# The first expert layer in 40 tiles instead of 47, eight of them shared by two experts, with the second down weights fetched from HBM

## The reference

```
logits = x @ router_weight.T + router_bias
top_val, top_idx = top_k(logits, 4);  top_val = softmax(top_val)
gate_up = einsum('th,ehd->etd', x, gate_up_proj) + gate_up_proj_bias
gate = min(gate, 7); up = clip(up, -7, 7); glu = gate * sigmoid(1.702 * gate)
out = einsum('etd,edh->eth', (up + 1) * glu, down_proj) + down_proj_bias
out = (out * router_scores).sum(experts)
```

## Time and profile before

| | |
|---|---|
| runs | 424.31, 425.56, 426.42 us (median 425.56) |
| span of the profiled execution | 422.5 us (first to last instruction; the page gives no time of its own for it beside the three runs) |
| TensorE busy | 407.8 us (97%) |
| VectorE busy | 330.4 us (78%) |
| ScalarE, POOL busy | 233.1 us, 216.9 us |
| layer one's tiles on TensorE | first gate/up at 39.15 us, last at 173.82 us |

### The profile page before, as it was taken

One profiled execution on the slowest core, in us unless ns is written; L12 is line 12 of the kernel. 1 busy time (PEld: TensorE's weight loads), 2 busy tenths in 40 slices (PEclk: granted clock), 3 DMA queues, 4 the chain that ended last, 5 costly groups with the idle time before them and its releaser, 6 DMA issues.

```text
span 422.5 us, 10072 instructions
## 1 busy us (share of the span) xinstructions
PE 407.8 (97%) x3213; PEld 321.5 (76%) x3213; DVE 330.4 (78%) x1121; ACT 233.1 (55%) x592; POOL 216.9 (51%) x208
## 2 busy tenths in 40 slices
PE   8999999999999999989999989999999999999995
PEld 4856999999999999856766668548877786565684
DVE  5876899999987666678999999847688774545896
ACT  3273233333433454589999972554777766633731
POOL 2114487888842322067786720067877740577710
PEclk9899999999999999969999999999999999999999
DMA  6947688889999998729977978023556553333322
GB/s 222 393 167 266 196 265 268 289 256 311 297 316 286 303 314 277 216 62 245 193 152 176 226 269 294 1 67 97 170 182 188 178 173 101 111 101 103 99 62 74
DMA packets 42275, 84.17 MB, mean 199 GB/s; under 512 B 7137, under 2 KB 27105, under 8 KB 41585
## 3 DMA queue, kind: packets, MB, share of 16 engines
q1 hardware_dynamic: 30656, 60.99, 44.1%
q0 software_dynamic: 9936, 20.85, 19.6%
q10 hardware_dynamic: 1632, 1.71, 1.2%
HBM read 65.81 MB, written 15.60 MB: 193 GB/s over the span
## 4 chain that ended last, share of the span: by engine, by line
PE 89%; DVE 7%; issue 2%; DMA 1%; ACT 1%; ACTq 0%; DVEq 0%
PE ps L1173 20%; PE ps L1189 9%; PE ps L1124 7%; PE ps L1370 7%; PE ps L1293 5%; PE ps L1151 5%; PE ps L1268 4%; PE ps L952 3%; PE ps L968 3%; PE ps L1381 3%; PE ps L1110 3%; PE ps L1162 2%; PE ps L971 2%; PE ps L941 2%; PE ps L1338 2%
## 5 line engine op out<-in xcount | busy, mean ns | idle before, releaser
L549 POOL DMA_INDIRECT til<-xn_rows,gidx x71 | 70.7, 996 | 86.4 <-PE ps L1162 38.9
L1173 PEld LDWEIGHTS ps<-til,experts 128*128 128x128 f32 x752 | 91.0, 192 | 3.7 <-issue 1.5
L1173 PE MATMUL ps<-til,experts 128*128 128x128 f32 x752 | 91.8, 275 | 0.1
L714 ACT ACTIVATE til<-ps 128x256 f32<-128x256 f32 x47 | 18.0, 383 | 69.8 <-PE ps L1162 69.8
L839 ACT ACTIVATE til<-til,mxs 128x128 f32<-128x128 f32 (+1 forms) x128 | 49.0, 452 | 0.0
L1189 PE MATMUL ps<-experts,til 128*128 x188 | 48.4, 381 | 0.0
L762 ACT ACTIVATE til<-ps,wtile 128x256 f32<-128x256 f32 x95 | 42.0, 468 | 3.7 <-PE ps L1153 2.4
L1795 DVE CUSTOM_DVE_ANT_0 til<-ps,cst 128x128 f32<-128x128 f32 (+1 forms) x128 | 37.8, 351 | 5.2 <-PE ps L1268 4.4
L1189 PEld LDWEIGHTS ps<-experts,til 128*128 128x128 f32 x188 | 32.1, 190 | 2.8 <-issue 0.3
L600 POOL DMA_INDIRECT rou<-sorted_rows,slotu x16 | 20.5, 1283 | 25.8 <-DMA sorted_rows<-til 19.4
L1126 PE MATMUL ps<-xn,til 128*64 128x192 f32 x192 | 33.8, 329 | 0.0
(11 more groups left out here) (247 smaller groups left out, 936.8 us busy)
## 6 DMA issues: line engine op xcount, KB each, us to landing
experts<-in_gu SPq DMA_DIRECT2D x47, 512.0 KB, 5.4
sorted_rows<-til SPq DMA_DIRECT2D x95, 128.0 KB, 1.9
experts<-in_gu SPq DMA_DIRECT2D x8, 768.0 KB
experts<-in_dn SPq DMA_DIRECT2D x4, 1024.0 KB, 12.4
experts<-in_dn SPq DMA_DIRECT2D x8, 384.0 KB
experts<-att SPq DMA_DIRECT2D x44, 32.0 KB
til<-xn_rows,gidx POOLq DMA_INDIRECT x71
xr<-in_x SPq DMA_DIRECT2D x2, 512.0 KB, 4.2
```

Of the source, the lines that this page charges most:

```text
L549: po.indirect_dma_start(to, None, xn_dram[s.n], bass.IndirectOffsetOnAxis(ap=gidx[:, t:t + 1], axis=0))\
L1173: mm = pe.matmul(ps[:, b0, m * P:(m + 1) * P], gw[:, j, k * w + m * P:k * w + (m + 1) * P], xgT[:, j % 2, k, :], start=(k == 0), stop=(k = ...
```

## The change

Layer one's slots are now rounded up to half tiles of 64 rows: NT0 = 40. 32 tiles hold one expert (WHOLE0). Eight hold two half tiles of two experts (MIXED0), for an expert whose last 64 rows or less are left over. They are taken in groups of five steps, the fourth of each group being the mixed one (tiles 3, 8, 13, ... 38 in the order of work; `tile_at` gives the place in the lists).

- A mixed tile takes two slots of gate/up weights, and is computed as rows: two bias matmuls with a one-hot column (`selc`) as the stationary side, then four matmuls of 64 rows by 512 columns. `gate_rows` is VectorE's part, `turn_rows_back` turns the result on TensorE at lag 3, `copy_rows` copies it to `hT` on ScalarE.
- `down` of a mixed tile has four matmuls of 64 rows. The first half's weights are read from `dn0_sb`, the second half's from `dn_other`, which SP fetches from HBM (256 KB) in `other_down(t)`, in iteration t.
- `gw` has six slots, and SP works five steps ahead instead of four. The two new slots lie in `att`, where `xnT0` was, so the second waits for the last wide projection.
- The routing gets the half tiles' arithmetic: six more operations in the chain, and a joint reduction that finds the owners of whole and half tiles.
- The hidden work moves: rotations at tiles 5, 8, 10, 13, 15, 18, 20, 23; heads at 14 to 24 and 25 to 35; the waits for the heads at 27 and 37; BIAS_TILE 28, and all its matmuls in bank 5.
- Semaphores are renamed or folded into the engines' chains (`s_tab`, `s_rst`, `s_rec`, `s_sil`, `s_x1n`, `h1_ready`); the waits stand where they stood.

The diff, cut to its core:

```diff
-NT0, NT1 = tiles_needed(E0, P), tiles_needed(E1, HALF_ROWS)
+NT0, NT1 = tiles_needed(E0, HALF_ROWS), tiles_needed(E1, HALF_ROWS)
+MIXED0 = E0 // 2
+WHOLE0 = NT0 - MIXED0
+STEPS0, MIXED_AT = 5, 3
+def mixed(i):
+    return i % STEPS0 == MIXED_AT
+def tile_at(i):
+    g, j = divmod(i, STEPS0)
+    return WHOLE0 + g if j == MIXED_AT else (STEPS0 - 1) * g + j - (j > MIXED_AT)
+def slots_at(i):
+    j = i % STEPS0
+    return (MIXED_AT, MIXED_AT + 1) if j == MIXED_AT else (j + (j > MIXED_AT),)
+        gw = [big[:, n * 1024:(n + 1) * 1024] for n in range(4)] + [att[:, n * 1024:(n + 1) * 1024] for n in (6, 7)]
+        dn_other = til[:, 3072:3584]
-        BIAS_TILE = 35
+        BIAS_TILE = 28
+        WEIGHT_TILE = 19
+        ROTATED = (5, 8, 10, 13, 15, 18, 20, 23)
+        HEADS_AT = (14, 25)
+        VALUES_AT = (27, 37)
...
+            def tile_weight(i):
+                g = i // STEPS0
...
+                if i >= STEPS0:
+                    sp.wait_ge(L[0].gu_done, i - STEPS0 + 1)
+                for n, j in enumerate(slots_at(i)):
+                    if g == 0 and j == 4:
+                        sp.wait_ge(L[0].wide_done, NTT)
+                    e = sp.snap(halves[g % 2][n] if mixed(i) else now[tile_at(i) % 4], min_val=0, max_val=E0 - 1)
+                    sp.dma_start(gw[j], gu0[:, bass.ds(e, 1), :].rearrange("p o n -> p (o n)")).then_inc(L[0].w_full[j], 16)
+            def other_down(i):
+                g = i // STEPS0
+                if g == 0:
+                    sp.wait_ge(L[0].lists, 3)
+                else:
+                    sp.wait_ge(L[0].y_done, i - STEPS0 + 1)
+                e = sp.snap(halves[g % 2][1], min_val=0, max_val=E0 - 1)
+                sp.dma_start(dn_other, dn0[:, bass.ds(e, 1), :].rearrange("p o n -> p (o n)")).then_inc(L[0].dn_full, 16)
...
                 for t in range(s.NT + 2):
-                    if s.n == 0 and t + 4 < s.NT:
-                        tile_weight(t + 4)
+                    if s.n == 0 and t + STEPS0 < s.NT:
+                        tile_weight(t + STEPS0)
+                    if s.n == 0 and t < s.NT and mixed(t):
+                        other_down(t)
                     if s.n == 0 and t == s.NT - 5:
                         weights_ahead()
-                    if s.n == 0 and (16 <= t < 27 or 28 <= t < 39):
-                        place_heads(t // 28, t - (16, 28)[t // 28])
+                    for half, at in enumerate(HEADS_AT if s.n == 0 else ()):
+                        if at <= t < at + 11:
+                            place_heads(half, t - at)
                     if t >= 2:
                         store(t - 2, (t - 2) % 4)
...
                 for t in range(4, s.NT):
                     gather(t)
-                    if s.n == 0 and t == 7:
+                    if s.n == 0 and t == ROTATED[0]:
                         po.wait_ge(s.lists, 3)
...
-                    if s.n == 0 and t in (33, 44):
-                        a = t // 44
+                    if s.n == 0 and t in VALUES_AT:
+                        a = VALUES_AT.index(t)
                         po.wait_ge(s_heads[a], 16 * 32)
...
+                def copy_rows(i, j):
+                    if not mixed(i):
+                        return
+                    ac.wait_ge(s.rows_turned, i // STEPS0 + 1)
+                    ac.wait_ge(s.y_done, i - 1)
+                    ac.activation(hT[:, j % 2, :, :], ps[:, 4, 0:D].rearrange("p (k t) -> p k t", k=KD), ACT.Copy).then_inc(s.rows_copied, 1)
...
+                    if mixed(t):
+                        h = 2 * tile_at(t)
+                        for c in range(2):
+                            pe.matmul(ps[c * HALF_ROWS:(c + 1) * HALF_ROWS, b0, :], selc[:, h + c:h + c + 1].broadcast_to([96, HALF_ROWS]), gub_bf, start=True, stop=False)
                     pe.wait_ge(s.xgT_ready, t + 1)
+                    for n in slots_at(t):
+                        pe.wait_ge(s.w_full[n], 16 * (t // STEPS0 + 1))
+                    if mixed(t):
                         for k in range(KD):
+                            for c, n in enumerate(slots_at(t)):
+                                rows = slice(c * HALF_ROWS, (c + 1) * HALF_ROWS)
+                                mm = pe.matmul(ps[rows, b0, :], xgT[:, j % 2, k, rows], gw[n][:, k * w:(k + 1) * w], start=False, stop=(k == KD - 1))
...
+                def turn_rows_back(t, j):
+                    if not mixed(t):
+                        return
+                    g = t // STEPS0
+                    pe.wait_ge(s.rows_gated, g + 1)
...
+                    for k in range(KD):
+                        mm = pe.transpose(ps[:, 4, k * P:(k + 1) * P], ubuf[:, j % 2, k * P:(k + 1) * P], ident)
+                    mm.then_inc(s.rows_turned, 1)
...
+                    if mixed(t):
+                        pe.wait_ge(s.rows_copied, g + 1)
+                        pe.wait_ge(s.dn_full, 16 * (g + 1))
+                        e = pe.snap(first_half[g % 2][0], min_val=0, max_val=s.E - 1)
+                        for k in range(s.KF):
+                            pe.matmul(ps[0:HALF_ROWS, 6 + j % 2, 0:D], hT[:, j % 2, k, 0:HALF_ROWS], dn[:, bass.ds(e * (s.KF * D) + k * D, D)],
+                                      start=(k == 0), stop=(k == s.KF - 1))
+                            mm = pe.matmul(ps[HALF_ROWS:P, 6 + j % 2, 0:D], hT[:, j % 2, k, HALF_ROWS:P], dn_other[:, k * D:(k + 1) * D],
+                                           start=(k == 0), stop=(k == s.KF - 1))
...
-                    run_tiles(s, [(1, 1, up), (0, 1, turn), (0, 4, experts), (0, 1, begin), (1, 1, weights), (1, 1, bias_rows), (3, 1, first_heads), (3, 1, down)])
+                    run_tiles(s, [(3, 1, turn_rows_back), (1, 1, up), (0, 1, turn), (0, 1, experts), (0, 1, begin), (1, 1, weights), (1, 1, bias_rows), (3, 1, first_heads), (3, 1, down)])
...
+                if s.n == 0:
+                    over = odd[:, 0:E]
+                    ve.tensor_tensor(over, ranks[:, NTT, :], nts[:, 0:E], ALU.is_gt).then_inc(s_dve, 1)
+                    ve.tensor_tensor(past, ranks[:, 0:NTT, :], nts[:, 0:E].unsqueeze(1).broadcast_to([P, NTT, E]), ALU.is_ge).then_inc(s_dve, 1)
...
+                    ve.tensor_tensor_scan(odds, ones_e[:, 0:E], over, -2.0 * NT0, ALU.mult, ALU.add).then_inc(s_dve, 1)
...
+                    link(ve.scalar_tensor_tensor(out=jump, in0=odds, scalar=-float(HALF_ROWS), in1=enda[:, 0:E], op0=ALU.mult, op1=ALU.subtract))
+                    ve.tensor_tensor(past, past, jump.unsqueeze(1).broadcast_to([P, NTT, E]), ALU.mult).then_inc(s_dve, 1)
...
+                    link(ve.tensor_tensor(lg, lg, past, ALU.add))
...
+                def gate_rows(t, j):
+                    ve.wait_ge(s.gu_done, t + 1)
+                    g, u = gbuf[:, j % 2, :], ubuf[:, j % 2, :]
+                    ve.tensor_scalar(g, ps[:, 2 + j % 2, 0:F], LIMIT, None, ALU.min).then_inc(s.g_ready, 1)
+                    ve.tensor_scalar(u, ps[:, 2 + j % 2, F:2 * F], 1.0, LIMIT + 1.0, ALU.add, ALU.min).then_inc(s.u_ready, 1)
+                    ve.wait_ge(s.u_ready, t + 1)
+                    link(ve.scalar_tensor_tensor(out=u, in0=u, scalar=1.0 - LIMIT, in1=g, op0=ALU.max, op1=ALU.mult))
+                    ve.wait_ge(s.sig_ready, t + 1)
+                    ve.scalar_tensor_tensor(out=u, in0=sig[:, j % 2, :], scalar=1.0, in1=u, op0=ALU.add, op1=ALU.mult).then_inc(s.rows_gated, 1)
```

More of the change, by code:

```diff
@@ L70, in constants @@
     c[:, C_HALF:C_HALF + 1] = 2 * (p % HALF_ROWS) + p // HALF_ROWS + 1
+    is_half = (p >= 2 * WHOLE0) & (p < 2 * NT0)
+    c[:, C_WHOLE:C_WHOLE + 1] = np.where(is_half, p // 2, p) + 1
+    c[:, C_ODD:C_ODD + 1] = np.where(is_half, -p, 1000)
     c[:, C_PART:C_PART + 1] = np.where((p >= 32) & (p < 96), -1.0, 0.0)
@@ L230, in build_program @@
         texi = sb("texi", [P, P], i32)
-        selc = sb("selc", [96, NT0], bf16)
-        bcol = sb("bcol", [P, 4, NT0])
+        selc = sb("selc", [96, 2 * NT0], bf16)
+        bcol = sb("bcol", [P, 4, WHOLE0])
+        odd = sb("odd_parts", [P, 4 * E0])
+        owner = sb("owners", [P, 2])
         wq = sb("wq", [P, NTT, 2, 3, 2], fp16)
@@ L299, in __init__ @@
                 if n == 0:
-                    self.w_full = [sem(f"gate_up_weights_{j}") for j in range(4)]
+                    self.w_full = [sem(f"gate_up_weights_{j}") for j in range(FETCHED)]
                     self.bcol_done = sem("bias_columns_picked")
@@ L798, in tiles @@
                 if s.n == 0:
-                    run_tiles(s, [(0, 1, turn), (0, 1, last_wide), (4, 1, weigh), (1, 1, gate), (1, 1, place_heads), (2, 1, bias_rows)])
+                    run_tiles(s, [(3, 1, copy_rows), (0, 1, turn), (0, 1, last_wide), (4, 1, weigh), (1, 1, gate), (1, 1, place_heads), (2, 1, bias_rows)])
                 else:
@@ L922, in _ @@
             before = [pe.alloc_register(f"expert_before{j}") for j in range(4)]
+            first_half = [[pe.alloc_register(f"first_half{g}_{j}") for j in range(2)] for g in range(2)]
```

(37 more changed lines are left out.)

177 lines of the change are left out of this document (95 added, 82 removed).

## The result

The changed kernel takes 455.99 us (median of 4 runs, 454.07 to 458.62) against 424.94 us (4 runs) for the kernel before: a ratio of 1.0734, 95% interval 1.0688 to 1.0779. That is slower by 31 us, where 16 were predicted, and it lies 1 us outside the range. The profiled execution's span is 453.8 us (before 422.5).

The account below looks back on a forecast made before the run. TensorE was taken as the bound, late arrivals adding one to one. Terms -20.1 + 7.8 + 1.4 + 15.6 + 8.0 + 0.8 + 2.5 = +16.0 us on 425.6 gave 441.6 us, range 427 to 455.

Parts of the forecast that it names:

- Tiles and mixed steps: Layer one on TensorE: seven steps of 2.87 us go, -20.1 us; eight mixed steps cost 0.97 more each, +7.8 us.
- Routing: Routing before the tiles: six more VectorE instructions, less smaller equality tables, delay TensorE's first list matmul by 1.4 us.
- The late fetch: Mixed tiles' down: second weights land late, TensorE waits 1.9 us at three tiles, 2.4 at four, 0.3 at one: +15.6 us.
- The clock: TensorE's granted clock falls after the idle time at `turn(38)`; 5 us at half speed cost +2.5 us.
- rival 3: TensorE's clock falls at every late fetch, 3.2 us each, seven make +22: 464 us; chance 0.10.
- The gather of tile 38: POOL waits for the heads before gathering this tile, so TensorE waits +8.0 us at `turn(38)`.
- The gather of tile 6: POOL's gather early in layer one: lands about when it is due, counted as nothing.
- Tile 28: Its gather comes late behind the heads: +0.8 us, or +3.2 if the fetch in step 26 is in time.
- Rival 2: Second down weights' fetch is in time, gathers behind the heads are not: +2.8 us, 428.4 us; chance 0.13.
- Rival 1: Fewer tiles pay: fetch lands before `down(t)`, heads early enough for tile 38; -10.9 us, 414.7 us; chance 0.12.

Follow-up runs that it names:

- the first run with filled idle time: The changed kernel with ten unused bf16 matmuls before TensorE's wait for the fetch in six mixed tiles: 452.21 us, ratio 1.0644 to the kernel before.
- the run with the early fetch: The changed kernel with the second down weights fetched two iterations earlier, ahead of that iteration's gate/up weights: 442.45 us, ratio 1.0399 to the kernel before.
- the version with everything in time: The changed kernel with the fetch two iterations earlier, GpSimd's head waits after tiles 31 and 39, heads before early loads, rotations from tile 7: 416.58 us.
- the copy: The version with everything in time, but ScalarE copies the second down weights from dn0_sb in place of the HBM fetch: 413.30 us, ratio 0.9733.

## Why the prediction was right in direction and short by half

1. **Tiles and mixed steps: right.** A whole step stayed at 2.87 us, and a cycle without waits is 15.33 us: 5 x 2.87 + 0.98, where 0.97 was predicted, from layer two's rows.
2. **Routing: too high.** VectorE's chain is 1.1 us longer, where 1.4 were predicted, but the first gate/up starts at 39.26 against 38.98 us. The step that failed is that TensorE "waits for VectorE's L1561 there". The bracket of the earlier trace rows names VectorE as the releaser, but VectorE's first table was done at 23.87 us (23.18 + 0.69) and TensorE loaded the list's weights at 25.03, behind matmuls that it had anyway: 1.16 us to spare. Now the table is done at 25.03 and the weights are loaded at 25.12, so the longer chain just fits. The 0.3 that are left lie within what the variants show, where the first gate/up starts between 38.66 and 39.55. Before, and after:

```profile
23.18 0.69 DVE L1561 TENSOR_TENSOR rou<-iota_mid,slot_mid 128x1024 f16<-128x1024 f16 x1
25.46 0.46 PE L1013 MATMUL ps<-til,rou 128*128 128x47 f16 x12
...
24.35 0.68 DVE L1688 TENSOR_TENSOR rou<-iota_mid,slot_mid 128x1024 f16<-128x1024 f16 x1
25.12 0.10 PEld L1073 LDWEIGHTS ps<-til,rou 128*128 128x128 f16 x1 [0.24 <-DVE rou L1688]
25.54 0.65 PE L1073 MATMUL ps<-til,rou 128*128 128x40 f16 x12
```

3. **The late fetch: right in mechanism, 15.6 us predicted, 18.8 measured.** At tile 8 issue (1.67 us into the step, predicted 1.8) and due time (5.25, predicted 5.24) were right. The landing was not: predicted at 7.1, it came at 8.3, and TensorE started at 8.55. Two terms of it were too small. The first gate/up weights, taken as there 4.3 us after their issue, took 5.7 at tile 8 and 4.6 at tile 13. "The second 512 KB and the fetch's 256 KB behind it need 1.28 and 0.64 us", together 1.92, at the 411 GB/s of a window with nothing but loads; they took 1.9 at tile 8, but 3.4 at tile 13 and 2.2 to 3.0 at the four behind it. While the fetch is under way, stores and gathers are under way too, and all of them together get 325 GB/s. Nor did the waits fall as the sum has them: tile 3, counted with 1.9, waits for nothing, since TensorE stood at `turn(6)` until 60.12 while the fetch landed at 58.6, and the four tiles with heads, put down from 3.3 to 2.4 each, waited 3.0 on average. By the limit of 358 GB/s that the Trainium skill gives (DMA: Bandwidth & Descriptors, Specifications) the waits would come to an estimated 19.1 us. Its total is the nearer one, but the kernel before moved 427 GB/s from 14 to 18 us, and a window of 1 us in the first run with filled idle time has 432, so it isn't that limit which was met. The Trainium skill (Perfetto Trace Analysis, Roofline) lets a core alone reach about 435 GB/s. With that the 427 and 432 agree. The landing of the first weights (L485) and of the fetch (L494), for tile 8 and for tile 13, and the window of the kernel before:

```profile
DMA to landing us min/median/max: 5.7/5.7/5.7
DMA to landing us min/median/max: 6.6/6.6/6.6
...
DMA to landing us min/median/max: 4.6/4.6/4.6
DMA to landing us min/median/max: 6.6/6.6/6.6
...
14.00:18.00 4.00, 4.00 (x13) 2.99 (x13) 3.55 (x28) 0.43 (x2) 0.00 (x0) 0.59 1.03 427
```

4. **The clock: the term that failed most.** Of the 13 us between the sum of +16 and the +29 added up above, 11.5 are here. I took +2.5 once and gave the fall at every late fetch a chance of 0.10. The reason given against it, that TensorE "is full before and after" the gap, was wrong: full work around it did not help. It fell after all six waits, and after both gathers: some +14 us. That is as rival 3 had it, but at 1.6 each, not 3.2, and beside waits larger than its sum counted.
5. **The gather of tile 38: 4.79, predicted 8.0.** The heads' way was as described: POOL waited 19.40 us for them.

```profile
190.70 0.20 POOL L617 MEMSET att<- 128x64 f32 x1 [19.40 <-DMA experts<-att]
190.79 0.91 POOL L618 MEMSET att<- 128x960 f32 x1
191.86 0.95 POOL L600 DMA_INDIRECT til<-xn_rows,gidx  x1 [0.16 <-issue]
```

   Against the start of step 37 (183.31) the gather went out at 8.55, predicted 10.0. The sync engine isn't held by TensorE's waits, and the last heads went out 0.19 us into that step (183.50), predicted 3.4; but POOL woke 7.2 us behind them, where 5.4 were taken. And the gather was due 1.9 us later, since that step ran mostly at half clock. The two make the 3.2 us. With the fetch in time it waits 9.55.
6. **The gather of tile 6: counted as nothing, 3.39 us and a fall of 1.6.** "The gather of tile 6 lands about when it is due" took a landing of about 2.7 us. POOL issued it at 54.25, behind the rotation of tile 5, while two weights and a fetch issued from 52.33 to 53.49 were under way, and TensorE could start on it only 5.9 us later.
7. **Tile 28: +0.8 predicted, none measured.** The waits of TensorE before it (four of them) gave the heads time. Without these it is 5.2 to 8.7 us, more than the 3.2 predicted for that case.

Rival 2 ("the fetch is in time, the gathers are not", 428.4) is the run with the early fetch: 442.45. It too was short by tile 28, by `turn(6)` and by the clock at each. Rival 1 (nothing late, 414.7) is the version with everything in time: 416.6, or 413.3 with the copy. The rivals' sums held where they had only TensorE's own work in them.

At the layer's end (its last down matmuls, at 208.75 against 179.26 us) the change is 29.5 us behind, at the end of the span 31.3. The version with everything in time loses 1.1 us there too. The granted clock is 0.50 for 10.2 us at the start of the attention, in both, against 6.8 us before. Whether that is the cause was not tried.

## What to carry to other kernels

Removing work from an engine that is the bound pays only if what it fetches keeps the old distance: count for each transfer how many bytes stand before it in its queue, and what else the DMA engines carry in that time, not the rate and the landing times of a quieter window. Price a wait of TensorE at its length plus what half the clock costs behind it. And when a wait is removed, look at once for the next thing that had been living from it: here the gathers, then the fetches themselves.

## What the runs showed of the hardware

- TensorE's granted clock fell to 0.50 behind every single wait of 2.32 us or more between full stretches of layer one (2.32 to 9.55 us, 31 of them in eight kernels), and behind none of the single waits up to 2.25 us (2.19, 2.20, 2.21 and 2.25 among them). These are too few to call the figure between them a limit: two short waits close together (0.64 and 1.20) also made it fall once, and at the start of the attention, with matmuls of 16 rows around it, it fell in every run within 3.1 us of a wait of 1.41, in some behind a second one of up to 1.00.
- Behind waits of up to 5 us it mostly came back 3 to 4 us after its fall, at 1.5 to 1.6 us lost. Six times it took near 7 us and cost 2.4 to 3.0 (behind waits of 3.05, 3.23, 3.60, 4.46, 4.79 and 4.99), while waits of 3.39, 3.66 and 3.88 cost 1.6: the length of the wait alone does not say which.
- A fetch of 256 KB behind 1 MB in the same queue landed after 6.6 us (5.1 to 7.0 in the seven of the change); first in its iteration it was there within 4.55 us at tile 8, but only after 6.64 at tile 18, beside the heads.
- With seven fetches of 256 KB more in the layer the time was 3.4 us longer; the DMA share of the windows was 1.03 and 1.00 with them, and 0.96 and 0.97 without.
